# Attention over head pairs: both batches of a pair in turn, one set of query weights for both

## The reference

```python
q = _rms_norm(x @ wq_a.T, q_norm_w) @ wq_b.T          # 32 heads of 128 + 64
kv = x @ wkv_a.T                                      # latent 64, rope key 64
kv_up = _rms_norm(kv_c, kv_norm_w) @ wkv_b.T          # per head: k_nope 128, v 128
scores = (einsum(q_nope, k_nope) + einsum(q_pe, k_pe)) * scale   # causal
out = einsum(softmax(scores), v) @ wo.T
x = x + attention(layernorm(x)) + ffn(layernorm(x))   # silu-gated ffn, 512 wide
```

## Time and profile before

| | us |
|---|---|
| runs | 1512.58, 1525.00, 1527.79 |
| the profiled execution | 1517.88 |
| its span | 1516.1 |
| TensorE busy, share of the span | 1320.1, 87% |
| VectorE busy | 1102.5, 73% |
| ScalarE busy | 955.1, 63% |
| GpSimd busy | 776.8, 51% |

### The profile page before, as it was taken

The page is one execution under the profiler, slowest core; times in us unless marked ns, Lnnn a source line. Parts: engine busy times, 40 slices in busy tenths (PEclk is TensorE's granted clock), DMA queues, the critical chain, the costliest instruction groups (busy, mean ns, idle before and its releaser), DMA issues. The chain is left out here.

```text
span 1516.1 us, 32860 instructions
## 1 busy us (share of the span) xinstructions
PE 1320.1 (87%) x13058; PEld 905.5 (60%) x13058; DVE 1102.5 (73%) x1664; ACT 955.1 (63%) x1690; POOL 776.8 (51%) x759
## 2 busy tenths in 40 slices
PE   4899995988989998999988899999889898479997
PEld 4787773666666666666666666666666666334443
DVE  3755454788888888888888888888888889542321
ACT  3644433777777777777777777777777778641120
POOL 0222011777677767767766776776776674000110
PEclk8999997999999999999999999999999999889999
DMA  4011004788899888799898888979888897799995
GB/s 158 29 56 57 28 21 138 136 161 145 155 173 171 163 147 157 157 162 173 153 161 152 155 159 163 167 159 172 141 161 154 157 168 139 178 182 228 247 244 131
DMA packets 573641, 225.85 MB, mean 149 GB/s; under 512 B 509232, under 2 KB 552880, under 8 KB 572848
## 3 DMA queue, kind: packets, MB, share of 16 engines
q1 hardware_dynamic: 562992, 199.09, 68.3%
q0 software_dynamic: 10496, 24.66, 7.2%
HBM read 55.91 MB, written 25.17 MB: 53 GB/s over the span
## 5 line engine op out<-in xcount | busy, mean ns | idle before, releaser
L737 ACT ACTIVATE prob_long_sb<-score_long,shift_sb 128x1024 f32<-128x1024 f32 (+3 forms) x256 | 245.0, 957 | 250.0 <-DVE shift_sb L853 249.8
L859 DVE TENSOR_TENSOR prob_hl_sb<-prob_long_sb,prob_hl_sb 128x1024 f16<-128x1024 f32 (+3 forms) x256 | 358.0, 1398 | 0.0
L853 DVE TENSOR_REDUCE shift_sb<-score_long 128x1 f32<-128x1024 f32 (+3 forms) x256 | 259.4, 1013 | 68.1 <-PE score_long L649 67.6
L828 POOL TENSOR_TENSOR ql_sb<-qf_sb,qh_sb 128x512 f16<-128x512 f32 x124 | 144.8, 1169 | 233.9 <-ACT qh_sb L757 233.9
L745 ACT ACTIVATE prob_hl_sb<-prob_long_sb 128x1024 f16<-128x1024 f32 (+3 forms) x256 | 232.5, 908 | 0.0
L646 PE MATMUL score_long<-key_hi,qh_sb 128*128 128x512 f16 (+3 forms) x512 | 176.3, 344 | 10.0 <-DVE ql_sb L914 9.1
L659 PE MATMUL flip<-ident_sb,prob_short_sb 128*128 128x128 f32 x640 | 117.4, 281 | 73.9 <-DVE ptl_short_sb L865 73.7
L845 POOL TENSOR_TENSOR qf_sb<-qf_sb,rot_sb 64x512 f32<-64x512 f32 x124 | 174.1, 1404 | 9.5
L821 POOL DMA_DIRECT2D rot_sb<-qf_sb x248 | 124.8, 508 | 104.6 <-DVE ql_sb L914 61.3
L680 PE MATMUL acc<-ch,prob_t_sb 128*128 128x65 f16 x1664 | 177.5, 192 | 0.0
L678 PE MATMUL acc<-ch,prob_t_sb 128*128 128x65 f16 x1664 | 177.2, 194 | 0.3 <-DMA prob_t_sb<-prob_hl_sb 0.3
(11 more groups left out here) (180 smaller groups left out, 3396.8 us busy)
## 6 DMA issues: line engine op xcount, KB each, us to landing
o<-o_sb SPq DMA_DIRECT2D x32, 512.0 KB, 4.5
o_nat_sb<-o SPq DMA_DIRECT2D x32, 512.0 KB, 6.8
rot_sb<-qf_sb POOLq DMA_DIRECT2D x248, 64.0 KB, 3.5
wqk_sb<-wqk SPq DMA_DIRECT2D x32, 320.0 KB, 4.4
wo_sb<-wo SPq DMA_DIRECT2D x16, 512.0 KB, 4.2
x_sb<-x SPq DMA_DIRECT2D x4, 1024.0 KB, 4.8
y<-y_sb SPq DMA_DIRECT2D x16, 256.0 KB, 2.0
wq_f_sb<-wqp SPq DMA_DIRECT2D x32, 128.0 KB, 4.5
```

The source lines that it names most:

```text
L737: nc.scalar.activation(prob[kind][:, s % 2, 0:width(s, kind)], score_of(s, kind), ACT.Exp, bias=shift[:, s % (2 * WIN), kind:kind + 1], sc ...
L853: nc.vector.tensor_reduce(shift[:, s % (2 * WIN), kind:kind + 1], score_of(s, kind), AX.X, ALU.min).then_inc(shift_ready[kind], 1)
L859: nc.vector.tensor_tensor(prob_hl[:, s % NHL, n:2 * n], prob[LONG][:, s % 2, 0:n], prob_hl[:, s % NHL, 0:n], ALU.subtract).then_inc(lo_rea ...
```

## The change

The order of the windows becomes pair 0 in batch 0, pair 0 in batch 1, pair 1 in batch 0, and so on: window w has pair `w // 2` and batch `w % 2`. The weights are formed once per pair. Those of pair 0 are formed before the first step. Those of pair 1 are formed in window 0, and those of pair p in window 2p - 3, thus in windows 1, 3, 5 to 27, at the same places in the window as before. The buffers of the weights go by the pair, and so do the loads. The output weights stay in every window.

```diff
+        def new_pair(w):
+
+            p = 1 if w == 0 else (w + 3) // 2 if w % 2 == 1 else PAIRS
+            return p if p < PAIRS else None
...
@@ sync
-                sp.dma_start(scr["o"][w % PAIRS, w // PAIRS], o[:, w % 2].rearrange("p t c -> p (t c)")).then_inc(o_out[w % 2], 16)
+                sp.dma_start(scr["o"][w // 2, w % 2], o[:, w % 2].rearrange("p t c -> p (t c)")).then_inc(o_out[w % 2], 16)
...
-            for j in range(2):
-                sp.wait_ge(wl_ready, j + 1)
-                load_w(2 + j)
+            sp.wait_ge(wl_ready, 1)
+            load_w(2)
...
-                if u == 3 and w + 4 < WINS:
-                    sp.wait_ge(wl_ready, w + 3)
-                    load_w(w + 4)
+                p = new_pair(w)
+                if u == 3 and p is not None and p + 2 < PAIRS:
+                    sp.wait_ge(wl_ready, p + 1)
+                    load_w(p + 2)
...
@@ tensor
-                b, j = p // PAIRS, p % 2
+                b, j = p % 2, p // 2 % 2
...
             absorb(0)
-            pe.wait_ge(lat_ready, 1)
-            absorb(1)
             pe.wait_ge(wl_ready, 1)
             for n in range(4):
                 project(n, score_long[:, n, :])
-            pe.wait_ge(wl_ready, 2)
...
-                            pe.wait_ge(wl_ready, n // 4 + 1)
+                            pe.wait_ge(wl_ready, n // 8 + 1)
...
-                        if w + 2 < WINS:
-                            absorb(w + 2)
+                        if new_pair(w) is not None:
+                            absorb(new_pair(w))
                         output_weights(w)
...
@@ scalar
-                    if w + 2 < WINS:
-                        weights_latent(w + 2)
+                    if new_pair(w) is not None:
+                        weights_latent(new_pair(w))
...
-                if high_weights_at(s) and w + 2 < WINS:
-                    weights_high(w + 2)
+                if high_weights_at(s) and new_pair(w) is not None:
+                    weights_high(new_pair(w))
...
@@ vector
-            for p in range(2):
-                weights_low(p)
+            weights_low(0)
...
-                if s < STEPS and high_weights_at(s) and w + 2 < WINS:
-                    weights_low(w + 2)
+                if s < STEPS and high_weights_at(s) and new_pair(w) is not None:
+                    weights_low(new_pair(w))
```

More of the change, by code:

```diff
@@ L545, in load_w @@
                 j = p % 2
-                sp.dma_start(raw[j][:].rearrange("p h c -> p (h c)"), io["wqk"][:, p % PAIRS, :]).then_inc(w_in[j], 16)
-                sp.dma_start(wf[j][:, :, KVL:KVL + 2 * ROPE], io["wqp"][:, p % PAIRS, :, :]).then_inc(w_in[j], 16)
+                sp.dma_start(raw[j][:].rearrange("p h c -> p (h c)"), io["wqk"][:, p, :]).then_inc(w_in[j], 16)
+                sp.dma_start(wf[j][:, :, KVL:KVL + 2 * ROPE], io["wqp"][:, p, :, :]).then_inc(w_in[j], 16)
             def load_wo(pair):
@@ L637, in scores @@
                 pair, head, i = s // WIN, s % WIN // BLK, tile(s, kind)
-                b = pair // PAIRS
+                b = pair % 2
                 q, row = slice(i * P, (i + 1) * P), 2 * (pair % 2) + head
@@ L662, in values @@
             def values(s):
-                b = s // WIN // PAIRS
+                b = s // WIN % 2
                 for kind in (SHORT, LONG):
@@ L771, in weights_high @@
                 nc.scalar.activation(wh[p % 2][:], wf[p % 2][:], ACT.Copy).then_inc(wh_ready, 1)
-            for p in range(2):
-                weights_latent(p)
-                weights_high(p)
+            weights_latent(0)
+            weights_high(0)
             for n in range(4):
```

## The result

The changed kernel takes 1468.8 us, the median of five runs (1464.79 to 1476.83); the kernel before, in five runs beside it, 1524.78 us (1512.58 to 1527.79). The ratio is 0.966, with an interval of 0.961 to 0.971: 3.4% less, some 52 us. A second set of runs gave 0.968 (0.962 to 0.973). The forecast was 1480 us.

A forecast was written before the change was run, and what follows sets the result against it. The prediction took VectorE and TensorE, handing work to each other in every step, to bound the kernel. Fifteen relieved windows at 2.81 us gave 42.1 us less, other terms zero: 1480 us from 1522, range 1465 to 1495.

The forecast's parts named there:

- The bracket above 50: Rival: TensorE sets the pace also in windows that keep their weights; gain more than 50 us, 60 at most; chance 0.04.
- relieved windows: The fifteen windows (2, 4 to 28, and 29) that stop forming weights: 30.13 us each, 2.81 less than 32.94.
- Steps 1 and 2: In a relieved window, without matmuls, rounding wait and subtraction: step 1 loses 0.91 us, step 2 loses 2.12, together 3.03.
- Step 3: In a relieved window it becomes like step 7: 4.21 us in place of 3.66, which costs 0.55.
- Step 4: In a relieved window it becomes like step 0: 4.34 us in place of 4.67, a gain of 0.33.
- Windows that form weights: Window 0 and odd ones to 27: zero change, TensorE's 0.73 us wait moving to its transposes; other bound 10 us.
- Before the first step: Second set's forming goes: zero taken, 0.2 us gain at most, up to 4.7 us lost if the clock rises later.
- The sum: Fifteen relieved windows at 2.81 us: 42.1 us less, attention about 999 us long.
- The overlap of GpSimd and VectorE that eats the gain: Rival: 0.87 us overlap on steps 1 to 3 of relieved windows; gain 3 us, 1519 us; chance 0.05.
- GpSimd's chain as the bound: Rival: GpSimd's query chain lags beyond its 1.07 us margin and TensorE stands at window starts; 1537 us; chance 0.02.
- The rule of the Trainium skill: Any GpSimd operation could hold back any VectorE subtraction; by it alone 1519 us; trace said to agree for step 3, not step 7.
- Step 7's fast subtraction: 768-wide VectorE subtraction in step 7, 1.07 us though it overlaps GpSimd's work, against 1.94 in step 3; held against the rule.

The follow-up runs named there:

- second profile: The changed kernel profiled once more, unaltered: 1472.5 us (median of four), ratio 0.968 to the kernel before.
- sine experiment: The changed kernel with GpSimd's sine multiplication cut from 512 to 448 columns: step 4 of relieved windows 4.44 us, these windows 30.10 us, attention 993.7 us.

## Why the prediction was right, and where not

**The number**: the measured 1468.8 us is 11 below the forecast, in the range but near its lower end. The prediction set that end with a gain of 47 us, though it speaks of 33 to 55; with 55 it would be 1458. By the ratio the gain is 52 us (45 to 59), and 35 to 50 was given a chance of 0.80. The bracket above 50 stood for shorter windows that form weights and a step 3 that keeps its length; neither was seen.

**What bounds the kernel**: right as far as it goes. VectorE and TensorE in turn, step by step. The DMA share is as high with faster windows, 0.87 over attention. But GpSimd is on the path too, through VectorE's subtractions: with most of its cosine work gone, relieved windows lose 0.44 us and the others 1.44.

**Steps 1 and 2** (0.91 and 2.12): right, 0.91 and 2.12 in the changed kernel's window 28.

**Step 3** (0.55 given back): right. It became step 7, 4.22 against 4.21.

**Step 4** (0.33 gained): this term was mis-sized, and it is 0.70 to 0.73. The model of the step was wrong, and it is luck that this cost only 0.4 us a window. I took step 0 as its model, at 4.34, with a 640-wide subtraction of 1.77 us in it. In step 0 GpSimd's addition starts first, in step 4 of a relieved window VectorE does, by 0.05 us. The sine experiment moved the order and got 4.44. The prediction had this mechanism as a loss among its rivals and not as a gain on the main path. With it a relieved window gives 3.15 to 3.18 us, fifteen of them 47.7, and not 42.1.

**Windows that form weights** (zero): right, 32.90 against 32.94, though the 0.73 us wait of the projection went. It came back at the transposes of step 4, as forecast.

**Before the first step** (zero, up to 4.7 lost): the first minimum comes at 257.4 and 255.5 us in two profiles, 259.2 before, and 256.6 in the kernel with the old number of weights in the new order. Nothing was lost, and what was gained is within that scatter. The clock rose no later than before: its mean between 241 and 242 us is 0.66 in the changed kernel and 0.50 in the kernel before.

**The sum**: attention should shorten by 42 us. It did by 48.1 in the second profile and by 44.1 in the first, which lost 5.0 in window 16. The medians differ by 51 to 56 us. The rest is start and last stage: the profile before, my base, had a last stage of 215.9 us, the shortest of all. Which part of those few microseconds the change has is open.

**The rivals.** The overlap of GpSimd and VectorE that eats the gain: the mechanism is real and has about the size given (0.87 us in an overlap; 1.06 in step 4), but its sign in step 4 was the other one. GpSimd's chain as the bound: not seen; between 480 and 1216 us TensorE waits for a remainder of the queries in no window. The rule of the Trainium skill (SBUF — State Buffer, SBUF: two separate sides), that GpSimd and VectorE take the shared ports as an exclusive lock for a whole instruction and that whoever starts first has it, fits these rows better than I gave it credit for: the held-back subtraction ends 1.95 to 1.97 us after the addition's start, however late it started. Step 7's fast subtraction, which I held against it, started 0.22 us before GpSimd's sine multiplication, and it was the latter that took long, 1.99 us; in window 16 above it takes 1.27. The short subtractions, one of whose inputs lies in PSUM, are not held back at all. This one runs while GpSimd is in its additions (1144.88 to 1147.97), and all 64 of its width in the changed kernel take 0.68 or 0.69 us:

```profile
1146.77 0.68 DVE L866 TENSOR_TENSOR ptl_short_sb<-flip,pth_short_sb 128x512 f16<-128x512 f32 x1
```

## What to carry to other kernels

Where two engines hand work to each other, price a removed operation by the step it stands in, and take the step's new length from a twin of it in the same trace that lacks the operation. Look there for other work whose duration depends on when it starts, and compare starts, not only lengths. After work has been taken out, ask what the new slack in due times allows: moving the rest into idle places gave 44 us more, nearly as much as leaving half of it out.

## What the runs showed of the hardware

- A VectorE subtraction with two SBUF inputs beside a GpSimd operation takes 0.82 or 1.88 us (640 columns), by who starts first. A shift of 0.13 us decided it, and less work on GpSimd made relieved windows slower by 0.35 us (and the others shorter by 0.27). With one input in PSUM (512 columns) it took 0.68 or 0.69 us every time.
- The one held back is not always VectorE: 1.27 us of GpSimd became 1.99. Once in twelve profiles VectorE was held through four of GpSimd's operations, for 5.05 us.
- Two costs measured by adding each back alone (1.37 and 2.43 us) exceeded the cost of both together (3.15), as each also spoiled the same later step.
